# Cross-attention and MX feed-forward on one core: values stored by head pairs through five staging tiles, their attention buffer refilled in six parts

## The chip, the cores and the metric

The kernel runs on one core of a Trainium2 chip, as one launch. The metric is the device time of the whole program in microseconds, as the median of several runs. A profile of one execution gives the trace that is read here. In it PE is TensorE's matmul stream, PEld its weight loads, DVE is VectorE, ACT ScalarE, POOL GpSimd and SP SyncE, which here only issues DMAs; SPq and ACTq are the DMA issues of SP and ACT.

## The reference, cut to what matters

x has 2048 rows of 512 (tokens), ctx has 6404 rows of 512 (4 x 1601 keys), and there are 16 heads of 32.

```
q  = layernorm(x) @ Wq + bq          # 2048 x 512, times 1/sqrt(32)
kv = ctx @ Wkv + bkv                 # 6404 x 1024: keys, values
q, k = fake_quant(q), fake_quant(k)  # int8, one scale for each row and head
v = fake_quant(v, axis=keys)         # int8, one scale for each of the 512 columns,
                                     # max|v| over all 6404 keys / 127
a = softmax(q k^T);  a = fake_quant_unsigned(a)   # uint8, one scale for each row
x = x + (a @ v) @ Wp + bp
x = x + mx_ffn(layernorm(x))         # 512 -> 2048 -> 512, block-scaled int8
```

The scale of a value column is known only when all 51 tiles of keys have been seen: no value can be rounded before the last one is projected.

## The kernel before, in words

There are three functions, each a block of its own in which the five engines run their own instruction streams and meet at semaphores; all engines finish one block before the next begins.

**prepare** walks through a list `ITEMS` of 67 items: 51 key tiles of 128 ctx rows (`KT` = 51, the last has 4 rows) and 16 query tiles. Queries 0 to 7 stand between key tiles 22 to 36, one at every second tile; queries 8 to 15 come last. For an item i, PE turns the input (`turn_in(i+1)`), multiplies (`project(i)`: keys into `ps_k`, values into `ps_v`, four f32 products of 512 columns each) and turns the previous item's result (`turn_out(i-1)`). For a key tile VectorE adds the bias, quantises by head (`split`, lines 568 to 578), and adds the bias to the values (`take_values`, line 591). The quantised keys are written as three bf16 parts: ScalarE copies the first (468), GpSimd subtracts (358), ScalarE copies the second (470), GpSimd subtracts again (361); PE turns all three (418), ScalarE copies them to `stage` (496, 497) and SP stores a pair of tiles to DRAM (282).

Values stay in SBUF as f32, in `v32`, a view of the whole `arena` (51 x 512 words a partition). The largest |v| is found by `largest_values` at 13 places (`GROUPS`), each a strided reduction over two to five tiles (599) and a maximum with `v_scale` (600). SP also stores columns of heads 4 to 15 of each tile to `late_v_dram`, by head pairs (`store_late_values`, 286). Beside the tiles VectorE prepares the FFN weights in 8 pieces, one in four tiles: `powers` at tiles 1, 5, .. 29 (609), `weight_bytes` one tile later (618), `weight_values` two later (624), 2.28 us each; and the biases in four steps at tiles 4, 6, 8 and 10 (554 to 563). `bias`, `w` and their parts lie in places of the arena that value tiles take over later.

After the last key tile, GpSimd reduces `v_scale` across partitions (367), VectorE forms `inv_v` (683, `scale_of_values`, at query 9), and beside queries 10 to 13 VectorE multiplies heads 0 to 3 (`EARLY_HEADS` = 4) by it into bytes (678, `value_bytes`), ScalarE widens them to f16 (522) and SP stores them (340). Before the block ends SP waits for all its stores.

**attention** has 256 rows of work (16 heads x 16 tiles of 128 queries). For each row PE makes 6404 scores in five chunks (833), VectorE copies each chunk out of PSUM with its maximum (888), GpSimd forms the row's maximum and bias (995, 999, 1003), ScalarE takes exp in two halves (940) as a byte part `n8` and a 16-bit part `n16`, SP transposes both by DMA (816, 820), GpSimd unpacks the bytes (1010, 1011) and PE multiplies by the values, three rows (`LAG`) behind the scores, in four parts between the score chunks (846). ScalarE takes the output (946).

At the beginning ScalarE's queue loads keys, queries and values of heads 0 and 1; later, at rows 0 to 5 of each head, keys (240 and 160 KB pieces) and queries of the next one (`next_head`, 910 and 914). Heads 4 to 15 get their values in f32 from `late_v_dram`, two heads (1632 KB) in one DMA into `late_v` at row 14 of heads 2, 4, .. 12 (`RELOAD_AT`, 933), and GpSimd multiplies and rounds them into `v_head` in six parts at rows 7 to 12 of the head before (1041, 1043, `round_values`), both operations of a part in one row and after that row's unpack. `SUMS_AT`, `INVERT_AT` and `SCALE_AT` (rows 2, 5 and 6) place the softmax sums, their reciprocals (VectorE, 896) and the scaling of the previous head's output (GpSimd, 1030).

**finish** does the projection and the FFN; the change leaves it as it is.

## Time and profile before

| | us |
|---|---|
| median of 3 runs | 2727.17 |
| lowest, highest | 2725.52, 2740.77 |
| the profiled execution | 2737.58 |
| its span from first to last instruction | 2735.8 |
| prepare, up to the next block's first instruction | about 553.7 |
| attention, first to last score copy | 564.6 to 2430 |
| finish | to 2735.8 |

The span is 1.8 us less than the profiled execution's time. Of the span VectorE is busy 2492.6 us (91%), PE 2249.1 (82%), ScalarE 1983.4 (72%) and GpSimd 1419.5 (52%). The mean granted TensorE clock is 0.821 of full speed. A stretch in which one engine is busy nearly all the time is bound by that engine; in the others a chain through several engines sets the pace, and it has to be followed tile by tile. Idle time of an engine that does not set the pace costs nothing.

### The profile page before, as it was taken

The page shows a single profiled execution, that of the slowest core. Times are in us where ns is not written, and L with a number is a line of the kernel's source. Part 1 is how long each engine was busy: PE and PEld are TensorE (multiplying, and loading weights), DVE is VectorE, ACT ScalarE, POOL GpSimd, SP SyncE. Part 2 cuts the span into 40 slices and gives each one's busy share as a digit, 9 for nine tenths or more (in the row PEclk, how much of TensorE's full clock was granted, in tenths as well). Part 3 has the DMA queues.
Part 4 walks back from the last instruction along what each step waited for, and adds up shares of the span by engine and source line. Part 5 has one row for each costly group of instructions (what it writes and reads, how often), then busy time and mean ns, then how long its engine had stood idle before and what let it go on. Part 6 is the DMA issues. An engine that isn't in the chain of part 4 may idle for free. (4 is left out here: it accounts for less than half of the span.)

```text
span 2735.8 us, 52956 instructions
## 1 busy us (share of the span) xinstructions
PE 2249.1 (82%) x20003; PEld 1193.3 (44%) x20020; DVE 2492.6 (91%) x3592; ACT 1983.4 (72%) x1813; POOL 1419.5 (52%) x1855
## 2 busy tenths in 40 slices
PE   8899899968888888788888788888887777867886
PEld 4444454424444444444444444444444444433443
DVE  6998667879999999999999999999999999957997
ACT  3344333458888888888888888888988888864665
POOL 2432222136556575666757667675775758552001
PEclk9999999967677777777777876787777888779999
DMA  7565445489999999999999999999999999991000
GB/s 228 123 146 114 89 97 120 90 190 175 197 177 202 203 181 197 181 197 185 191 210 180 193 200 193 192 183 211 178 197 194 189 195 175 180 213 43 16 16 27
DMA packets 1389368, 442.13 MB, mean 162 GB/s; under 512 B 1323924, under 2 KB 1364372, under 8 KB 1387576
## 3 DMA queue, kind: packets, MB, share of 16 engines
q1 hardware_dynamic: 1378472, 397.08, 76.7%
q10 hardware_dynamic: 10736, 43.11, 6.3%
q8 instruction: 76, 1.25, 0.2%
q14 instruction: 84, 0.69, 0.1%
HBM read 78.99 MB, written 42.35 MB: 44 GB/s over the span
## 5 line engine op out<-in xcount | busy, mean ns | idle before, releaser
L888 DVE TENSOR_SCALAR_CACHE_REDUCE arena<-a_ps_s 128x1281 f32<-128x1281 f32 (+1 forms) x1280 | 1826.3, 1488 | 46.1 <-PE a_ps_s L833 38.1
L940 ACT ACTIVATE arena<-arena,a_bias,a_row_scale 128x3328 uint8<-128x3328 f32 (+1 forms) x512 | 1560.4, 3048 | 257.4 <-POOL a_bias L1003 255.7
L833 PE MATMUL a_ps_s<-arena,a_q_rep 96*128 96x512 bf16 (+2 forms) x3840 | 1232.4, 443 | 325.0 <-DVE arena L888 290.7
L846 PEld LDWEIGHTS a_ps_o<-a_v_head,a_nT 128*128 128x128 f16 x13056 | 529.6, 103 | 295.2 <-issue 160.9
L833 PEld LDWEIGHTS a_ps_s<-arena,a_q_rep 96*128 (+1 forms) x3840 | 314.6, 109 | 767.8 <-DVE arena L888 417.8
L1010 POOL CAST a_nT<-arena 128x1664 int16<-128x1664 uint8 x256 | 401.8, 1570 | 352.3 <-DMA arena<-arena 349.5
L846 PE MATMUL a_ps_o<-a_v_head,a_nT 128*128 128x32 f16 x13056 | 518.8, 183 | 43.4 <-POOL a_nT L1011 39.8
L1011 POOL CAST a_nT<-arena 128x1664 int16<-128x1664 uint8 x256 | 402.9, 1574 | 0.0
L358 POOL TENSOR_TENSOR p_rest<-p_kq,p_parts 128x512 f32<-128x512 f32 (+1 forms) x51 | 88.8, 1742 | 317.2 <-ACT p_parts L468 317.2
L999 POOL TENSOR_SCALAR a_row_max<-a_row_max,a_part_max 128x1 f32<-128x1 f32 x256 | 92.2, 360 | 246.6 <-DVE arena L888 229.3
L388 PE MATMUL p_ps_k<-p_wkv,p_ctxT 128*128 128x512 f32 (+1 forms) x408 | 190.3, 611 | 0.0
L388 PE MATMUL p_ps_v<-p_wkv,p_ctxT 128*128 128x512 f32 (+1 forms) x408 | 183.4, 592 | 0.0
L468 ACT ACTIVATE p_parts<-p_kq 128x512 bf16<-128x512 f32 (+1 forms) x51 | 32.1, 630 | 187.7 <-DVE p_kq L578 114.0
L1168 POOL TENSOR_TENSOR f_o<-arena,f_y 128x512 f32<-128x512 f32 x16 | 18.5, 1154 | 236.4 <-DVE f_y L1377 236.4
L388 PEld LDWEIGHTS p_ps_v<-p_wkv,p_ctxT 128*128 128x128 f32 (+1 forms) x408 | 76.7, 188 | 98.4 <-issue 98.2
L388 PEld LDWEIGHTS p_ps_k<-p_wkv,p_ctxT 128*128 128x128 f32 (+1 forms) x408 | 75.9, 197 | 78.1 <-issue 78.1
L568 DVE TENSOR_TENSOR p_kf<-p_ps_k,p_bkv 128x512 f32<-128x512 f32 (+1 forms) x51 | 35.2, 690 | 80.7 <-PE p_ps_k L388 80.1
L995 POOL TENSOR_SCALAR a_row_max<-a_part_max 128x1 f32<-128x1 f32 x256 | 93.6, 366 | 27.9 <-DVE arena L888 26.3
L888 DVE DVE_READ_ACCUMULATOR arena<-a_ps_s 128x1 f32 x1280 | 105.9, 83 | 0.0
L470 ACT ACTIVATE p_parts<-p_rest 128x512 bf16<-128x512 f32 (+1 forms) x51 | 32.1, 630 | 94.5 <-POOL p_rest L358 94.5
L940 ACT ACTIVATION_READ_ACCUMULATOR arena<-arena,a_bias,a_row_scale 128x1 f32 x512 | 95.7, 187 | 0.0
L1043 POOL TENSOR_SCALAR a_v_head<-a_late_v 128x256 f16<-128x256 f32 x72 | 82.8, 1150 | 6.7
(151 smaller groups left out, 1943.0 us busy)
## 6 DMA issues: line engine op xcount, KB each, us to landing
k_parts_transposed<-p_stage SPq DMA_DIRECT2D x25, 768.0 KB, 7.0
p_ctx<-in_ctx_dram SPq DMA_DIRECT2D x25, 512.0 KB, 5.8
arena<-k_parts_transposed ACTq DMA_DIRECT2D x48, 240.1 KB, 4.0
late_values<-arena SPq DMA_DIRECT2D x51, 192.0 KB, 6.9
a_late_v<-late_values ACTq DMA_DIRECT2D x6, 1632.0 KB, 9.6
arena<-in_L_ffn_W_dram SPq DMA_DIRECT2D x8, 1024.0 KB, 8.1
arena<-k_parts_transposed ACTq DMA_DIRECT2D x48, 160.1 KB, 3.8
a_q_rep<-q_transposed ACTq DMA_DIRECT2D x48, 128.0 KB, 5.4
```

The source lines that it names most:

```text
L358: nc.gpsimd.tensor_tensor(rest1[0:r, :], kq[0:r, :], parts[0:r, 0, :], ALU.subtract).then_inc(rest_ready, 1)
L388: last = nc.tensor.matmul(out, ctxT[:, i % 2, j, 0:r], weights[:, j], start=(j == 0), stop=(j == CC - 1))
L568: nc.vector.tensor_tensor(kf[0:r, :], ps_k[0:r, i % 2, :], bkv[0:r, 0:C], ALU.add).then_inc(k_taken, 1)
L833: last = nc.tensor.matmul(ps_s[:, b, n0:n0 + w], q, k_parts[0:3 * HD, slot, start[c] + n0:start[c] + n0 + w], start=True, stop=True)
L846: last = nc.tensor.matmul(ps_o[:, u, 0:HD], nT[:, u, j, :], v_head[:, v_slot, j, :], start=(j == 0), stop=(j == KT - 1))
L888: nc.vector.tensor_scalar(s_row[:, u, start[c]:start[c] + size[c]], ps_s[:, (u + c) % 2, 0:size[c]], 1.0, None, ALU.mult, ALU.max, accum_o ...
L940: nc.scalar.activation(out, s_row[:, u, keys_of_half[half]], ACT.Exp, scale=row_scale[:, u, 0:1], bias=bias[:, u:u + 1], accum_out=zsum[:, ...
L995: nc.gpsimd.tensor_scalar(m, part_max[:, u, 0:1], part_max[:, u, 1:2], part_max[:, u, 2:3], ALU.max, ALU.max).then_inc(three_done, 1)
L999: nc.gpsimd.tensor_scalar(m, m, part_max[:, u, 3:4], part_max[:, u, 4:5], ALU.max, ALU.max).then_inc(row_max_ready, 1)
L1010: nc.gpsimd.tensor_copy(low_T[u], bytes_T[:, u, :, 0])
L1011: nc.gpsimd.tensor_copy(high_T[u], bytes_T[:, u, :, 1]).then_inc(unpacked, 1)
L1043: nc.gpsimd.tensor_scalar(v_head[:, h % 2, tiles, :], some, ROUND, ROUND, ALU.add, ALU.subtract).then_inc(v_rounded, 1)
```

## The change

**Values.** `v32`, `GROUPS` and `late_values` go. A tile of values is written to one of five staging tiles (`v_tile`, `V_TILES` = 5) and stored whole, 512 columns as eight head pairs, to one DRAM tensor `v_dram` (`store_values`). ScalarE makes |v| of each tile (`vabs`, ACT.Abs) between its two copies of the key parts, and VectorE takes the maximum of it and `v_scale` one tile later (`largest_value`), 51 times. VectorE waits for the store and the Abs of tile t-5 before it writes tile t.

**Biases.** The third part is subtracted for one partition only, straight into `b_parts`: one copy less.

**Early heads.** `EARLY_HEADS` becomes 2. After all values are stored SP loads the first pair (`v_first`, 1632 KB) back; bytes are made at queries 10 and 11, ScalarE widens them straight into `v_head`, which together with `q_rep` now exists in both blocks. SP loads the keys of heads 0 and 1 at queries 9 and 10, the first half of their queries at 11 and 12, and head 0's second half at the end, before the block ends; `k_parts` moves to the beginning of the arena. `qiT` gets four tiles instead of two.

**Attention.** PE waits for 96 instead of 144 at heads 0 and 1, whose rows 4 to 15 are written out instead of looped, with a wait for the second half of the queries at row 8. The loads of heads 0 and 1 at the block's beginning shrink to the second half of head 1's queries; heads 2 and 3 load there as six parts. The reload becomes six DMAs of a sixth (272 KB), at rows 5, 7, 9, 11, 13 and 15 of heads 2, 4, .. 12. GpSimd does one of the 12 rounding operations in each of rows 3 to 14, before the row's unpack. The reciprocals move to row 7 and the scaling to row 15.

```diff
-EARLY_HEADS = 4
 GROUP = 2
+EARLY_HEADS = GROUP
...
+            def store_values(t):
+                sp.wait_ge(v_taken, t + 1)
+                sp.dma_start(v_dram[:, :, place(t), :].rearrange("g p c -> p g c"),
+                             v_tile[:, t % V_TILES, :].rearrange("p (g c) -> p g c", c=GROUP * HD)).then_inc(
+                                 v_stored[t % V_TILES], 16)
...
             for t in range(2 * PAIRS - 2, KT):
-                store_late_values(t)
+                store_values(t)
+            for i in range(V_TILES):
+                sp.wait_ge(v_stored[i], 16 * ((KT + V_TILES - 1 - i) // V_TILES))
+            sp.wait_ge(b_stored, 16)
+            sp.wait_ge(w_bytes, PIECES)
+            sp.dma_start(v_first.rearrange("p t c -> p (t c)"),
+                         v_dram[0].rearrange("p t c -> p (t c)")).then_inc(v_first_loaded, 16)
+
             for t in range(HALF_Q, QT):
-                if t > HALF_Q:
-                    store_query(t - 1)
...
+                store_query(t)
+                if t == HALF_Q + 1:
+                    sp.wait_ge(k_stored[0], 16 * ((PAIRS + 2) // 2))
+                    sp.wait_ge(k_stored[1], 16 * ((PAIRS + 1) // 2))
+                if HALF_Q + 1 <= t <= HALF_Q + 2:
+                    load_keys(t - HALF_Q - 1)
...
+                if HALF_Q + 3 <= t <= HALF_Q + 4:
+                    load_queries(t - HALF_Q - 3, 0, head_loaded[t - HALF_Q - 3])
+            for i in range(Q_TILES):
+                sp.wait_ge(q_stored[i], 16 * (QT // Q_TILES))
+            load_queries(0, 1, late_q_loaded[0])
...
                 nc.scalar.activation(parts[0:r, 0, :], kq[0:r, :], ACT.Copy).then_inc(hi_ready, 1)
+                act.wait_ge(v_taken, t + 1)
+                after_first(act, vmax_done, t - 1)
+                nc.scalar.activation(vabs[0:r, t % 2, :], v_tile[0:r, t % V_TILES, :], ACT.Abs).then_inc(vabs_ready, 1)
                 act.wait_ge(rest_ready, t + 1)
...
             def take_values(t):
                 r = rows(t)
-                if t == BIAS_TILE:
-                    dve.wait_ge(b_stored, 16)
-                if t == W_TILE:
-                    dve.wait_ge(w_turned, 2 * PIECES)
+                if t >= V_TILES:
+                    dve.wait_ge(v_stored[t % V_TILES], 16 * (t // V_TILES))
+                    dve.wait_ge(vabs_ready, t - V_TILES + 1)
...
-            def largest_values(t):
-
-                for first, last in GROUPS.get(t, ()):
-                    some = v32[:, first:last, :].rearrange("p t c -> p c t")
-                    dve.wait_ge(v_taken, t + 1)
-                    steps.then_wait(nc.vector.tensor_reduce(largest[:], some, AX.X, ALU.max, apply_absolute_value=True))
-                    steps.then_wait(nc.vector.tensor_tensor(v_scale[:], v_scale[:], largest[:], ALU.max))
...
+            def largest_value(t):
+                r = rows(t)
+                dve.wait_ge(vabs_ready, t + 1)
+                after_first(dve, vmax_done, t)
+                nc.vector.tensor_tensor(v_scale[0:r, :], v_scale[0:r, :], vabs[0:r, t % 2, :],
+                                        ALU.max).then_inc(vmax_done, 1)
...
-    ROUND_AT, ROUND_PARTS, RELOAD_AT = 7, 6, 14
...
+    ROUND_AT, ROUND_PARTS = 3, 6
+    RELOAD_AT = [ROUND_AT + 2 + 2 * part for part in range(ROUND_PARTS - 1)] + [QT - 1]
...
+            def load_late_values(group, part):
+
+                after_first(act, v_rounded, ((group - 1) * GROUP - 1) * ROUND_PARTS + part + 1 if group > 1 else 0)
+                tiles = slice(part * KT // ROUND_PARTS, (part + 1) * KT // ROUND_PARTS)
+                act.dma_start(late_v[:, tiles, :].rearrange("p t c -> p (t c)"),
+                              v_dram[group, :, tiles, :].rearrange("p t c -> p (t c)")).then_inc(late_v_loaded, 16)
...
             for row in range(ROWS):
-                maximum_and_unpack(row, row % 2)
-                head, part = row // QT + 1, row % QT - ROUND_AT
-                if EARLY_HEADS <= head < H and 0 <= part < ROUND_PARTS:
-                    round_values(head, part)
+                maximum(row, row % 2)
+                head, step = row // QT + 1, row % QT - ROUND_AT
+                if EARLY_HEADS <= head < H and 0 <= step < 2 * ROUND_PARTS:
+                    round_values(head, step)
+                if row >= 1:
+                    unpack(row - 1, 1 - row % 2)
```

## Rows read from the trace of the kernel before

**Rows 1.** Windows: stretch, its length, then busy us of PE, PEld, DVE, ACT, POOL.
```profile
56.75:207.56 150.81, 136.49 (x577) 71.02 (x576) 137.44 (x175) 66.09 (x92) 55.81 (x33) 0.95 0.59 136
207.56:395.77 188.21, 170.83 (x705) 88.39 (x704) 131.59 (x201) 74.72 (x114) 48.69 (x32) 0.96 0.48 104
395.77:509.31 113.54, 111.66 (x440) 54.25 (x438) 86.51 (x139) 42.37 (x71) 32.80 (x28) 1.00 0.49 101
564.62:2430.00 1865.38, 1518.43 (x16791) 825.08 (x16789) 1829.03 (x2575) 1599.87 (x1279) 1218.61 (x1706) 0.76 1.03 190
```

**Rows 2.** One line's view, L888 within attention (its waits), L820 (ns min/median/max).
```profile
  PE a_ps_s L833: 27.3, 21
...
L820 SPq DMA_TRANSPOSE a_nT<-arena x256: 3699/3828/11876, 580.2 to 2436.1; - x128
```

**Rows 3.** Timeline: start, us, instruction, [idle before]; SP and VectorE in attention.
```profile
1145.77 10.96 SPq L820 DMA_TRANSPOSE a_nT<-arena  x1
...
1161.01 1.49 DVE L888 TENSOR_SCALAR_CACHE_REDUCE arena<-a_ps_s 128x1281 f32<-128x1281 f32 x1 [5.66 <-PE a_ps_s L833]
```

**Rows 4.** Groups of instructions by line: busy us, mean ns, idle before, releaser.
```profile
L1010 POOL CAST a_nT<-arena 128x1664 int16<-128x1664 uint8 x256 | 401.8, 1570 | 352.3 <-DMA arena<-arena 349.5
L1043 POOL TENSOR_SCALAR a_v_head<-a_late_v 128x256 f16<-128x256 f32 x72 | 82.8, 1150 | 6.7
L599 DVE TENSOR_REDUCE p_largest<-arena 128x512 f32<-128x2048 f32 (+3 forms) x13 | 46.3, 3561 | 0.4
L470 ACT ACTIVATE p_parts<-p_rest 128x512 bf16<-128x512 f32 (+1 forms) x51 | 32.1, 630 | 94.5 <-POOL p_rest L358 94.5
L600 DVE TENSOR_TENSOR p_v_scale<-p_v_scale,p_largest 128x512 f32<-128x512 f32 x13 | 9.0, 693 | 0.4
L508 ACT ACT_TABLE_LOAD x1 | 1.3, 1283 | 0.0
```

**Rows 5.** Timeline of VectorE: the first instruction of key tiles 35 and 37.
```profile
374.84 0.69 DVE L568 TENSOR_TENSOR p_kf<-p_ps_k,p_bkv 128x512 f32<-128x512 f32 x1 [2.42 <-PE p_ps_k L388]
...
395.77 0.69 DVE L568 TENSOR_TENSOR p_kf<-p_ps_k,p_bkv 128x512 f32<-128x512 f32 x1 [2.42 <-PE p_ps_k L388]
```

**Rows 6.** Groups of PE by line, up to 505 us: its transposes of the key parts.
```profile
L418 PE MATMUL p_ps_t<-ident,p_parts 128*128 128x128 bf16 x596 | 44.3, 227 | 33.5 <-ACT p_stage L497 25.6 <-POOL p_parts L361 7.9
```

**Rows 7.** Timeline of PE in prepare: the same 12 transposes behind two waits.
```profile
130.53 0.84 PE L418 MATMUL p_ps_t<-ident,p_parts 128*128 128x128 bf16 x12 [0.92 <-ACT p_stage L497]
...
276.71 1.46 PE L418 MATMUL p_ps_t<-ident,p_parts 128*128 128x128 bf16 x12 [6.64 <-ACT p_stage L497]
```

**Rows 8.** Timeline of VectorE and GpSimd near tiles 7 and 8.
```profile
79.96 2.28 DVE L624 SCALAR_TENSOR_TENSOR arena<-arena,p_power 128x2048 bf16<-128x2048 int8 x1
...
80.06 3.20 POOL L358 TENSOR_TENSOR p_rest<-p_kq,p_parts 128x512 f32<-128x512 f32 x1 [3.12 <-ACT p_parts L468]
...
87.90 1.16 POOL L358 TENSOR_TENSOR p_rest<-p_kq,p_parts 128x512 f32<-128x512 f32 x1 [2.75 <-ACT p_parts L468]
```

**Rows 9.** One line's view, DMA landing: the last value stores (L286), then `late_v` (L933).
```profile
DMA to landing us min/median/max: 4.6/5.0/5.5
...
DMA to landing us min/median/max: 7.7/9.6/13.0
```

**Rows 10.** Timeline of SP's queue at the end of prepare.
```profile
514.11 2.02 SPq L286 DMA_DIRECT2D late_values<-arena  x3
```

**Rows 11.** Timeline of VectorE: end of prepare, beginning of attention.
```profile
524.52 1.86 DVE L678 TENSOR_TENSOR p_ctx<-arena,inv_v 128x1632 int8<-128x1632 f32 x1
...
545.88 0.69 DVE L664 TENSOR_TENSOR p_kf<-p_ps_k,p_bq 128x512 f32<-128x512 f32 x1 [0.87 <-PE p_ps_k L388]
...
553.73 0.16 DVE L892 MEMSET arena<- 128x124 uint32 x1 [2.43 <-PEq L57]
...
564.62 1.50 DVE L888 TENSOR_SCALAR_CACHE_REDUCE arena<-a_ps_s 128x1281 f32<-128x1281 f32 x1 [10.73 <-PE a_ps_s L833]
```

**Rows 12.** DMA issues of the page: KB each, median us to landing.
```profile
arena<-k_parts_transposed ACTq DMA_DIRECT2D x48, 240.1 KB, 4.0
```

More of the change, by code:

```diff
@@ L965, in rows_of_head @@
                         next_head(h + 1, 1 - slot, t)
+            later = slice(T // 2, T)
             for s in range(3):
-                for half in range(2):
-                    load(0, 0, s, half)
-            load_values(0, 0)
-            for s in range(3):
-                for half in range(2):
-                    load(1, 1, s, half)
-            load_values(1, 1)
+                act.dma_start(q_rep[s * HD:(s + 1) * HD, 1, later], q_dram[HD:2 * HD, later]).then_inc(late_q_loaded[1], 16)
+            for part in range(ROUND_PARTS):
+                load_late_values(1, part)
             act.dma_start(wp[:], A.wp.rearrange("(j p) n -> p j n", p=P)).then_inc(wp_loaded, 16)
@@ L1011, in unpack @@
                 nc.gpsimd.tensor_copy(high_T[u], bytes_T[:, u, :, 1]).then_inc(unpacked, 1)
-            def maximum_and_unpack(row, u):
-                maximum(row, u)
-                if not (isinstance(row, int) and row == 0):
-                    unpack(row - 1, 1 - u)
             def add_sums(h):
```

192 lines of the change are left out of this document (92 added, 100 removed).

## The prediction

> **What bounds the kernel.** I read the stretches first [rows 1]. The kernel has three parts: prepare up to about 553.6 us, attention from 564.6 to 2430, and the rest, which the change does not touch. In attention VectorE is busy 1829 of 1865 us: it copies each score chunk out of PSUM, and nothing in the change alters that. What can be won there is only what VectorE waits for PE inside it: 27.3 us in 21 waits [rows 2]. Two of them are over 5 us, each some rows after a 1632 KB reload of `late_v`; ahead of the one of 5.66 SP was 10.96 us at issuing one transpose [rows 3], whose median is 3.8 [rows 2]. GpSimd waited 352.3 us for transposes in all [rows 4], 1.4 a row.
>
> In prepare PE and VectorE share the bound. From 395.77 to 509.31 there are 14 key tiles, 8.1 us each. From 56.75 to 207.56 there are 16 tiles, where that pace would give 130 us and 150.81 were taken [rows 1]. Two tiles and a query take 20.93 us when undisturbed [rows 5]; the 16 tiles and 8 queries from 207.56 to 395.77 would take 167.4 at that pace and took 188.21. So 21 + 21 = 42 us are lost. PE waits in its transposes of the key parts 33.5 us [rows 6], the longer times behind tiles in which VectorE does its split, a grouped maximum of 3.6 us on average [rows 4] and a piece of the weights. PE also runs slower just after: the same 12 transposes take 1.46 us behind a wait of 6.64 and 0.84 behind one of 0.92 [rows 7], so a wait costs more than its length.
>
> **Part 1, the maximum of |v|.** Removed: 13 reductions, 46.3 us, and 13 small maxima of 693 ns, 9.0 us [rows 4]. Added on VectorE: 51 maxima of the same kind at 0.69, 35 us. VectorE so has 20 us less, and, more important, no tile with 3.6 to 5.4 us extra. In the first stretch it loses four such groups (of 4.7 or 3.8 us and 0.7 each, near 20 us) and gains 16 x 0.72 = 11.5: busy 137.4 becomes some 129 of a PE bound of 130. Bubbles remain, since the bias steps and weight pieces still make tiles of near 12 us: I take 140, 11 us less. In the second stretch VectorE's 131.6 busy us are far below 167; its two bad places are two reductions that each meet a weight piece, one with 6.64 us of PE waiting [rows 7]. I take 5 of the 21 us lost to stay: 16 less. After 395.77 there is little to win. Sum -27; from nothing (the chain is the bound, not VectorE) to -42 (everything lost comes back).
>
> Added on ScalarE: 51 Abs of 128x512. The nearest row is the copy of the same shape, 630 ns; ScalarE waits 94.5 us for GpSimd's difference right behind the place of the Abs [rows 4], 1.85 a tile, and the Abs fits in. It also waits for `v_taken`, which VectorE gives 0.7 us after the keys that ScalarE has just copied. Cost 0; if that cover were gone 51 x 0.63 = 32 us. Bound above: an Abs that needed a table load of 1.28 us [rows 4] before and after it: 2.6 us where 1.2 are free, 51 x 1.4 = 71. I take 0, since copies and a square root in prepare share one set. The Trainium skill ("ScalarE: Activation LUTs", Table sets) says that abs is in every set, so by it there is no load; no row here shows an Abs.
>
> Against the change: each new maximum has two SBUF inputs and falls on GpSimd's differences. GpSimd's subtraction takes 1.16 us beside a reduction, and 3.20 beside a VectorE operation of 2.28 us with two SBUF inputs [rows 8]; so a 0.69 us maximum can cost it 0.7. The chain from a key tile to PE's transposes (3.4 us split, copy 0.63, difference 1.2, copy 0.63, difference 1.2, handshakes) is about 8 us, PE's way to the same place (values, next keys and values, 3.6 each, and a transpose) 11.4. It holds 0.7 more, and with a weight piece (+2) just so. I charge nothing and keep up to 10 us of the gain as uncertain. The Trainium skill says the same ("GPSIMD Engine Reference", Key points: GpSimd shares its SBUF interfaces with VectorE, contention with instructions of two SBUF inputs); by it every tile pays the 0.7, and 51 x 0.7 = 36 us would be its worst, if PE waited for all of it.
>
> **Part 2, staging and stores.** Value tile t is overwritten by t+5 and stored about two tiles after it is made; the last three stores land in 4.6 to 5.5 us [rows 9], two or more tiles before the place is wanted. SP's store has a third more pieces; what is queued behind on SP (weights, queries, context) has tiles of slack. Cost 0; a store late by more than two tiles would stop VectorE. The bias edit drops one copy, counted as nothing.
>
> **Part 3, the end of prepare.** Before, VectorE makes head 0's bytes at 524.52 [rows 11]. Now they wait for all stores (the last issues end at 516.1 [rows 10], landing takes 5, a third larger: 522.3) and for a 1632 KB load. The nearest transfers of that size land in 7.7 to 13.0 us, beside transposes [rows 9]; here the queues are idle, so 8: 530.3. Behind VectorE's wait stand queries 11 to 15, and PE and ScalarE wait for those. Bytes 1.9 and query 11 to 535.3, bytes and query 12 to 540.2; PE comes from idle and is slow at first (I add 1.7, in the proportion of [rows 7]); then 4.2 a query: query 15 begins near 551.5 instead of 545.88 [rows 11]. That is +5.6, with 3 and 12 as bounds. SP issues three query loads before the barrier: +1. Two fewer heads of bytes are already inside.
>
> Then the gain: the block begins at 553.7 and the first score copy at 564.62, behind 10.73 us of waiting [rows 11]. PE's first products need about 1.3 us; heads 0 and 1 are now loaded before the barrier, by SP between the last queries. -9.4. Net 5.6 + 1 - 9.4 = -3; range -6 to +5.
>
> **Part 4, attention.** The 1632 KB transfer becomes six of 272 KB, at rows 5, 7, 9, 11, 13 and 15 of even heads. Each should hold the transposes a sixth of what the whole did, near 1.7 us instead of 10, and PE's lag of three rows absorbed 4 to 5 us of the large one. At row 5 it stands beside a key load of the next head; key pieces of 240 KB land in 4.0 us [rows 12] and the waits after them are 1.5 us at most. ScalarE issues it behind a wait on `v_rounded` that GpSimd has met one row before, so it blocks nothing. Rounding moves from both operations (a multiplication, and the rounding of 1.15 us [rows 4]) in six rows, after the unpack, to one in each of twelve, ahead of it: it falls into the 1.4 us a row in which GpSimd waits for the transpose. Heads 2 and 3 join: 24 operations of at most 1.15, under 28 us, hidden the same way. The scaling of a head moves from the crowded row 6 to row 15.
>
> Of 27.3 us about 18 follow a reload, 9 the key loads. I leave 10: -17, from -24 to 0. The Trainium skill ("DMA: Bandwidth & Descriptors", Rules for kernel authors) speaks against it: coalesce small transfers, at least 1 MiB for bandwidth. By that the six would hold the engines longer than the one; in rows: 6 x 4.0 = 24 us against 9.6.
>
> **Sum.** -27 - 3 - 17 = -47. The profiled execution took 2737.6 us and would take 2691; the median of the runs is 2727.2, so I forecast 2727 - 47 = 2680.
>
> **Rivals.**
> - *Chain (0.15).* GpSimd's stretched differences become PE's bound wherever a weight piece runs; prepare gives 8 instead of 27. For it: the 3.20 us of [rows 8]. Against: at those tiles the early chain already carries +2 without a PE wait. 2727 - 28 = 2699.
> - *Reload costs the same in pieces (0.12).* The 10 us of a reload are only spread, and the added traffic of heads 2 and 3 counts. -27 - 3 = -30: 2697.
> - *Six transfers cost more (0.05, the other side).* In each of 36 rows the transfer stops transposes for up to its whole 4.0 us landing. A row has 7.3 us (1865 / 256), SP's two transposes take 3.8 and, by my estimate, under half of that: some 5.5, so 1.8 are free; the rest, 2.2, comes to 36 x 2.2 = 79, less the 30 of the other parts: +49, 2776. It is slower than before when a transfer costs over 30 / 36 = 0.8 us. The coalescing rule above would lead here.
> - *First values late (0.05).* The load of the first pair takes 13 us and the stores land later: the end of prepare gives +5 instead of -3: 2688.
> - *The change moves nothing in prepare or attention (0.01).* 2724.
> - *The Abs loads tables (0.01).* 2680 + 71 = 2751.
>
> **Numbers.** The forecast holds 0.61. The range reaches from -72 (all bounds good: 42 + 6 + 24) cut to 2655, to 2708, which takes in the first two rivals and part of the worst; outside are about 2 in 10. A measurement of this kernel can tell about 1% (27 us) from no change. Faster by over 1%: the forecast, most of the late load, and over half of the first two rivals: 0.81. Within 1%: 0.14. Slower: 0.05.
>
> **What will show it.** Right: the first query after tile 50 starts near 482 instead of 509; no PE wait over 3 us in the key transposes; VectorE idle 5 to 8 us before head 0's bytes; first score copy 1.5 us after the block begins; VectorE's waits in attention near 10 us with none over 3; no transpose issue over 6 us. Wrong: GpSimd's differences with medians near 1.9 us and PE still waiting behind them; VectorE waiting at the value copy; waits of VectorE at rows 6 to 16 of even heads, one for each reload.

## The result, and the profile after

The changed kernel takes 2688.8 us (median of 4 runs, 2682.2 to 2691.2), the kernel before 2729.5 in the same series (4 runs, 2725.5 to 2740.8): ratio 0.984, 95% interval 0.9805 to 0.9876. It is 40.7 us faster, 1.5 %. Forecast were 47 us less, and 2680 us. In a second series the same two kernels had 2682.2 and 2725.1: 42.9 us less, ratio 0.9845 (0.980 to 0.9891).

The windows of the changed kernel, in the columns of [rows 1] (the last three numbers of a row are the granted clock, the share of the DMA engines and GB/s). The stretches are cut at the same work: key tiles 5 to 21, 21 to 37, 37 to the first query behind tile 50, the rest of prepare, attention, the rest of the program.

```profile
55.58:195.84 140.26, 134.73 (x581) 70.28 (x580) 133.34 (x182) 73.81 (x106) 55.80 (x32) 0.99 0.63 154
195.84:370.21 174.37, 164.35 (x702) 84.15 (x701) 129.38 (x209) 85.80 (x133) 50.93 (x33) 1.00 0.52 118
370.21:481.75 111.54, 111.50 (x440) 54.36 (x438) 80.09 (x145) 49.72 (x84) 34.16 (x28) 1.00 0.50 111
481.75:530.00 48.25, 32.69 (x132) 15.85 (x133) 30.70 (x63) 15.93 (x28) 2.05 (x3) 0.91 0.68 154
530.00:2381.00 1851.00, 1489.04 (x16791) 818.47 (x16789) 1827.13 (x2575) 1601.00 (x1279) 1238.69 (x1729) 0.79 1.06 192
```

Against [rows 1] the first two stretches (key tiles 5 to 21 and 21 to 37) are 10.6 and 13.8 us shorter, and PE's granted clock in them rose from 0.95 and 0.96 to 0.99 and 1.00; the third is 2.0 shorter. In attention VectorE is as busy as before (1827.13 against 1829.03); what it lost is idle time.

| stage, us | before | after | change | forecast |
|---|---|---|---|---|
| up to the query behind tile 50 | 509.31 | 481.75 | -27.6 | -27 |
| from there to the first score copy | 55.31 | 48.25 | -7.1 | -3 |
| attention, first score copy to its end | 1864.4 | 1849.7 | -14.6 | -17 |
| the rest | 306.8 | 306.4 | -0.4 | 0 |
| span | 2735.8 | 2686.2 | -49.6 | -47 |

The profiled executions differ by 49.6 and the medians by 40.7. The larger part of the difference is that the profiled execution of the kernel before lay above the median of its runs (experiment 12 profiles it again).

The end of prepare, from the timeline of VectorE of the changed kernel (start, us, instruction, idle before); compare [rows 11]:

```profile
499.67 1.86 DVE L696 TENSOR_TENSOR arena<-arena,inv_v 128x1632 int8<-128x1632 f32 x1 [2.60 <-DMA arena<-values]
...
519.39 0.69 DVE L681 TENSOR_TENSOR p_kf<-p_ps_k,p_bq 128x512 f32<-128x512 f32 x1 [0.88 <-PE p_ps_k L406]
...
528.79 0.16 DVE L917 MEMSET arena<- 128x124 uint32 x1 [3.37 <-PEq L57]
530.00 1.49 DVE L913 TENSOR_SCALAR_CACHE_REDUCE arena<-a_ps_s 128x1281 f32<-128x1281 f32 x1 [1.05 <-PE a_ps_s L853]
```

VectorE waits 2.60 us for head 0's values. Query 15 (519.39) begins 37.6 us behind the first query, before 36.6. The block begins at 528.79, and the first score copy waits 1.05 us instead of 10.73.

### The profile page after: what moved, and what is told of

The parts are those of the page before. It is cut to its first block and busy times, and to the rows that moved or that the text cites. A ratio compares the mean times of both kernels' runs of the same rounds, so it can differ in the third digit from the quotient of the medians.

```text
span 2686.2 us, 53043 instructions
## 1 busy us (share of the span) xinstructions
PE 2212.1 (82%) x20020; PEld 1181.0 (44%) x20020; DVE 2478.9 (92%) x3614; ACT 2009.7 (75%) x1862; POOL 1443.9 (54%) x1879
## 5 line engine op out<-in xcount | busy, mean ns | idle before, releaser
L913 DVE TENSOR_SCALAR_CACHE_REDUCE arena<-a_ps_s 128x1281 f32<-128x1281 f32 (+1 forms) x1280 | 1824.3, 1488 | 23.7 <-PE a_ps_s L853 16.6
L853 PE MATMUL a_ps_s<-arena,q_rep 96*128 96x512 bf16 (+2 forms) x3840 | 1201.6, 434 | 345.6 <-DVE arena L913 313.9
L853 PEld LDWEIGHTS a_ps_s<-arena,q_rep 96*128 (+1 forms) x3840 | 310.7, 108 | 782.8 <-DVE arena L913 456.5
L866 PEld LDWEIGHTS a_ps_o<-v_head,a_nT 128*128 128x128 f16 x13056 | 524.3, 102 | 263.6 <-issue 148.5
L866 PE MATMUL a_ps_o<-v_head,a_nT 128*128 128x32 f16 x13056 | 514.1, 182 | 28.9 <-POOL a_nT L1027 26.2
L1026 POOL CAST a_nT<-arena 128x1664 int16<-128x1664 uint8 x256 | 401.8, 1569 | 211.1 <-DMA arena<-arena 205.7
L376 POOL TENSOR_TENSOR p_rest<-p_kq,p_parts 128x512 f32<-128x512 f32 (+1 forms) x51 | 74.9, 1469 | 286.0 <-ACT p_parts L486 286.0
L1011 POOL TENSOR_SCALAR a_row_max<-a_part_max 128x1 f32<-128x1 f32 x256 | 93.8, 366 | 15.5 <-DVE arena L913 14.9
L379 POOL TENSOR_TENSOR p_parts<-p_rest,p_parts 128x512 bf16<-128x512 f32 (+1 forms) x51 | 81.0, 1588 | 37.7 <-ACT p_parts L491 37.7
L1057 POOL TENSOR_SCALAR v_head<-a_late_v 128x256 f16<-128x256 f32 x84 | 96.6, 1150 | 7.1
```

The costliest lines, as they stand in the source:

```text
L376: nc.gpsimd.tensor_tensor(rest1[0:r, :], kq[0:r, :], parts[0:r, 0, :], ALU.subtract).then_inc(rest_ready, 1)
L379: nc.gpsimd.tensor_tensor(parts[0:r, 2, :], rest1[0:r, :], parts[0:r, 1, :], ALU.subtract).then_inc(lo_ready, 1)
L853: last = nc.tensor.matmul(ps_s[:, b, n0:n0 + w], q, k_parts[0:3 * HD, slot, start[c] + n0:start[c] + n0 + w], start=True, stop=True)
L866: last = nc.tensor.matmul(ps_o[:, u, 0:HD], nT[:, u, j, :], v_head[:, v_slot, j, :], start=(j == 0), stop=(j == KT - 1))
L913: nc.vector.tensor_scalar(s_row[:, u, start[c]:start[c] + size[c]], ps_s[:, (u + c) % 2, 0:size[c]], 1.0, None, ALU.mult, ALU.max, accum_o ...
L1011: nc.gpsimd.tensor_scalar(m, part_max[:, u, 0:1], part_max[:, u, 1:2], part_max[:, u, 2:3], ALU.max, ALU.max).then_inc(three_done, 1)
```

## Experiments

Twelve kernels ran. `q8` is the start of the query behind tile 50. "Attention" goes from the first score copy to the end of the last. "Waits" are VectorE's idle time ahead of its score copies, behind the first copy; all but at most 0.6 us of each sum are waits for PE. "Time" is a median; kernels of one series share the runs of the kernel before: 2725.1 for experiments 1, 2, 4 and 5, 2732.6 for 6 to 9, 2724.8 for 3, 10 and 11, and 2726.2 for 12. The ratio is taken against these. The median of the same kernel before moves by 8 us between the series, so a few us between two kernels of different series say nothing; what a stage costs is read from the traces.

| kernel | q8 | first score copy | attention | waits | time | ratio |
|---|---|---|---|---|---|---|
| before | 509.3 | 564.6 | 1864.4 | 27.3 | 2729.5 | |
| 12 before, again | 508.2 | 563.5 | 1855.2 | 19.6 | 2726.9 | 1.000 (0.998 to 1.003) |
| after | 481.8 | 530.0 | 1849.7 | 16.0 | 2688.8 | 0.984 (0.981 to 0.988) |
| 1 changed, again | 483.3 | 531.9 | 1836.6 | 4.5 | 2682.2 | 0.985 (0.980 to 0.989) |
| 2 one reload | 483.1 | 531.4 | 1859.5 | 24.9 | 2697.3 | 0.989 (0.984 to 0.993) |
| 3 one reload, again | 482.4 | 529.7 | 1861.2 | 24.2 | 2701.8 (1 run) | |
| 4 rounding behind | 483.5 | 531.7 | 1844.6 | 12.2 | 2681.4 | 0.983 (0.979 to 0.987) |
| 5 reload later | 484.0 | 532.1 | 1839.5 | 6.8 | 2678.1 | 0.982 (0.978 to 0.986) |
| 6 maximum alone | 482.8 | 537.4 | 1853.3 | 17.7 | 2702.3 | 0.990 (0.983 to 0.997) |
| 7 no maximum | 483.5 | 531.8 | 1841.8 | 9.6 | 2679.0 (2 runs) | 0.980 (0.972 to 0.989) |
| 8 maximum ahead | 491.1 | 539.0 | 1839.0 | 5.4 | 2688.2 | 0.984 (0.977 to 0.990) |
| 9 loads in attention | 484.5 | 539.9 | 1847.9 | 13.0 | 2693.6 | 0.985 (0.978 to 0.991) |
| 10 weight halves | 489.7 | 537.0 | 1840.4 | 7.2 | 2686.8 | 0.986 (0.983 to 0.990) |
| 11 halves, reload later | 492.1 | 539.2 | 1835.5 | 3.4 | 2684.2 | 0.985 (0.983 to 0.988) |

### 1 to 3: the changed kernel again, and with one reload

Experiment 1 is the changed kernel unedited.

> The changed kernel itself, beside the experiments on one chip. Its first profile had VectorE waiting for PE 16 us within attention, 12.9 of them near row 8 of heads 4, 6, 8, 10 and 12 (2.21, 4.29, 1.23, 2.70, 2.51). If these come from a fixed meeting of transfers, a second profile shows waits at the same rows, 10 to 18 us in sum. If they are chance, they lie elsewhere. Ratio to the kernel before 0.984.

It has 4.5 us of waits, 1.8 of them near row 8 of even heads, where the first execution had 16.0 and 12.9: less than either theory had. The ratio repeats (0.9845). The waits of one execution are one sample, so they are compared below as groups.

Experiment 2 gives the reload back as one transfer of 1632 KB, at row 15 of even heads (the kernel before has it at row 14). The waits on it follow, and the first load of heads 2 and 3 is one transfer too; all else stays. Experiment 3 is the same kernel again.

```diff
-    RELOAD_AT = [ROUND_AT + 2 + 2 * part for part in range(ROUND_PARTS - 1)] + [QT - 1]
+    RELOAD_AT = [QT - 1]
...
-                tiles = slice(part * KT // ROUND_PARTS, (part + 1) * KT // ROUND_PARTS)
+                tiles = slice(0, KT)
```

> The changed kernel with the reload of a pair as one DMA of 1632 KB again, at row 15 of even heads; rounding stays spread over twelve rows. Theory (one large transfer holds up the transposes): waits of 4 to 7 us near row 2 of odd heads come back, waits near row 8 of even heads go, VectorE's waits in attention 25 to 30 us instead of 16, time +10 us. Rival (the spread rounding, not the split transfer, made attention shorter): waits stay near 16 us, time the same within 3.

> A second look at the changed kernel with one DMA of 1632 KB at row 15. Waits differ between executions of one kernel, so the sums have to be compared as groups: so far 27.3, 17.7 and 24.9 us with one transfer, and 16.0, 4.5, 12.2, 9.6, 5.4 and 13.0 with six. Theory: 18 to 28 us again, most of it at rows 2 to 4 of odd heads. Rival (the groups overlap by chance): under 14.

The waits are back, 24.9 us against 4.5, and the time with them: 2697.3 (2694.3 to 2699.8) against 2682.2 (2678.7 to 2691.4), 15 us. The third kernel repeats it: 24.2 us. In both they lie behind the reload again, at rows 2 to 4 of the odd heads (about 17 and 16 us of the sum); in the kernel before, whose reload is one row earlier, they begin at row 1. The worst of them, in the timeline of SP's queue, ScalarE's queue, PE and VectorE of experiment 3:

```profile
1578.00 0.34 ACTq L953 DMA_DIRECT2D a_late_v<-values  x1
1581.83 10.52 SPq L840 DMA_TRANSPOSE a_nT<-arena  x1
...
1594.82 0.53 PE L866 MATMUL a_ps_o<-v_head,a_nT 128*128 128x32 f16 x13 [6.61 <-POOL a_nT L1026]
...
1596.54 1.49 DVE L913 TENSOR_SCALAR_CACHE_REDUCE arena<-a_ps_s 128x1281 f32<-128x1281 f32 x1 [6.71 <-PE a_ps_s L853]
```

The transfer is issued at 1578.00, the next long transpose takes SP 10.52 us instead of its median of 3.85, GpSimd's unpacked row is late, PE waits 6.61 and VectorE 6.71. The part of the change that pays in attention is the six transfers, not the spread rounding. Experiments 1 and 2 share a series, and their runs don't overlap.

### 4: rounding behind the unpack

```diff
+                if row >= 1:
+                    unpack(row - 1, 1 - row % 2)
                 head, step = row // QT + 1, row % QT - ROUND_AT
                 if EARLY_HEADS <= head < H and 0 <= step < 2 * ROUND_PARTS:
                     round_values(head, step)
-                if row >= 1:
-                    unpack(row - 1, 1 - row % 2)
```

> The changed kernel with each rounding step behind the row's unpack instead of ahead of it. Theory (the step only fills GpSimd's wait for the transpose, and GpSimd has time either way): GpSimd's wait before the unpack goes from 206 us back to about 330, and the time moves by less than 3 us. Rival (the place of rounding is worth part of the gain): VectorE's waits in attention grow from 16 to 25 us, time +8.

No difference: 2681.4 (2677.9 to 2684.3) against 2682.2. GpSimd's wait ahead of its unpack is 343.5 us here and 211.1 in the changed kernel, where the rounding lies inside it; VectorE notices neither.

### 5: reload later

The waits left over in the first profile of the changed kernel lie near row 8 of even heads: 12.9 of the 16.0 us. The largest, from the timeline:

```profile
1269.99 0.34 ACTq L953 DMA_DIRECT2D a_late_v<-values  x1
...
1270.37 0.59 ACTq L935 DMA_DIRECT2D arena<-k_parts_transposed  x1
1271.00 0.82 ACTq L939 DMA_DIRECT2D q_rep<-q_transposed  x1
...
1273.00 8.47 SPq L840 DMA_TRANSPOSE a_nT<-arena  x1
...
1281.02 1.57 POOL L1026 CAST a_nT<-arena 128x1664 int16<-128x1664 uint8 x1 [6.85 <-DMA arena<-arena]
...
1285.96 1.49 DVE L913 TENSOR_SCALAR_CACHE_REDUCE arena<-a_ps_s 128x1281 f32<-128x1281 f32 x1 [4.29 <-PE a_ps_s L853]
```

The reload's first piece (row 5) goes out 0.4 us ahead of a key load and 1.0 ahead of a query load of the next head. The transpose behind all three takes 8.47 us, and VectorE waits 4.29 us, three rows on. So the pieces were moved to rows with fewer loads beside them:

```diff
-    RELOAD_AT = [ROUND_AT + 2 + 2 * part for part in range(ROUND_PARTS - 1)] + [QT - 1]
+    RELOAD_AT = [7, 9, 10, 12, 14, 15]
```

> The changed kernel with the six reloads at rows 7, 9, 10, 12, 14 and 15 instead of 5, 7, 9, 11, 13 and 15, so that none stands beside a key load of rows 0 to 5. Theory (the waits near row 8 of even heads come from the reload at row 5 on top of the key loads, and from the one at row 7 before the backlog is gone): these waits fall from 12.9 us to under 4, time 8 to 10 us less than the changed kernel. Rival (each reload costs by itself wherever it stands): the waits move with the reloads to rows 10 to 15 and keep their sum.

The waits near row 8 are 0.2 us here and 1.2 in experiment 11; in the seven executions with a piece at row 5 they lie between 1.8 and 12.9. 6.8 us remain in all, spread over other rows. Forecast were 8 to 10 us less time. The time is 2678.1 (2677.2 to 2680.4), the lowest of all, but its 4 us below experiment 1 are within that one's own spread: the waits near row 8 are gone, a gain in time isn't shown.

### 6: the maximum alone

Part 1 of the change put into the kernel before: Abs on ScalarE, a maximum per tile on VectorE; staging, end of prepare and attention as before.

```diff
+                nc.scalar.activation(vabs[0:r, t % 2, :], v32[0:r, place(t), :], ACT.Abs).then_inc(vabs_ready, 1)
...
-                    steps.then_wait(nc.vector.tensor_reduce(largest[:], some, AX.X, ALU.max, apply_absolute_value=True))
-                    steps.then_wait(nc.vector.tensor_tensor(v_scale[:], v_scale[:], largest[:], ALU.max))
+                nc.vector.tensor_tensor(v_scale[0:r, :], v_scale[0:r, :], vabs[0:r, t % 2, :],
+                                        ALU.max).then_inc(vmax_done, 1)
```

> The kernel before with the maximum of |v| by tile alone (Abs on ScalarE, one maximum on VectorE in each tile), everything else as before. Theory: this is the whole gain in the key tiles: the first query after the last key tile starts at 482 to 485 us instead of 509.3, attention keeps its 27 us of waits, time -25 us. Rival (staging tiles, w-waits and the bias edit also carry part of it): it starts at 490 or later, time -15 or less.

q8 lies at 482.8: the whole gain of the key tiles is this part's, and staging, stores and the bias edit carry nothing, as forecast. The time is 30 us below the kernel before, where 25 were expected; attention has 17.7 us of waits and not 27, which is in the spread of the kernel before itself (experiment 12).

### 7 and 8: how much the new maximum still costs

Experiment 7 lets the maximum work on one column of 512 and leaves the others out of the scales (`v_scale` starts at 1 there). Each of the 51 maxima still takes 0.16 us instead of 0.69. Experiment 8 puts the maximum of tile t - 1 ahead of tile t's split instead of behind its values.

```diff
-                nc.vector.tensor_tensor(v_scale[0:r, :], v_scale[0:r, :], vabs[0:r, t % 2, :],
+                nc.vector.tensor_tensor(v_scale[0:r, 0:1], v_scale[0:r, 0:1], vabs[0:r, t % 2, 0:1],
...
-            nc.vector.memset(v_scale[:], 0.0).then_inc(set_up, 1)
+            nc.vector.memset(v_scale[:], 1.0).then_inc(set_up, 1)
```

> The changed kernel with the per-tile maximum over one column instead of 512, so that v_scale is left out of the computation; Abs stays. It gives the floor of what the maximum costs. Theory (VectorE's load in the first 16 tiles still sets them): tiles 5 to 21 take 130 to 133 us instead of 140.3, tiles 21 to 37 167 to 170 instead of 174.4, GpSimd's second difference falls from 1.59 to about 1.2 us. Rival (what is left there is the bias steps and the weight pieces): tiles 5 to 21 stay at 137 or more.

```diff
+                if t >= 1:
+                    largest_value(t - 1)
                 split(t)
                 take_values(t)
-                if t >= 1:
-                    largest_value(t - 1)
```

> The changed kernel with the maximum of tile t-1 at the beginning of tile t, ahead of its split, instead of behind its values: VectorE does the same work, but GpSimd's second difference no longer meets it in light tiles. Theory (contention with GpSimd is hidden by the chain's slack): L379's mean falls from 1588 to about 1250 ns and the key tiles end within 2 us of before. Rival (the contention is on PE's path): the key tiles end 5 to 8 us earlier.

Both expectations missed. Without the maximum tiles 5 to 21 take 137.3 instead of 140.9 (130 to 133 were expected), tiles 21 to 37 take 177.7 instead of 174.4, and q8 is where it was: 27 us less of VectorE's work won nothing. With the maximum ahead, tiles 5 to 21 take 140.4, tiles 21 to 37 182.0, and q8 is 7.7 us late. GpSimd's second difference fell there as expected, from 1588 to 1351 ns, but the first rose from 1469 to 1686. The timelines of one place, tile 22, show why. First the changed kernel:

```profile
208.63 0.68 DVE L618 TENSOR_TENSOR p_v_scale<-p_v_scale,arena 128x512 f32<-128x512 f32 x1
...
208.98 1.35 POOL L376 TENSOR_TENSOR p_rest<-p_kq,p_parts 128x512 f32<-128x512 f32 x1 [5.44 <-ACT p_parts L486]
209.23 3.24 DVE L635 SCALAR_TENSOR_TENSOR arena<-arena,p_inverse 128x2048 int8<-128x2048 f32 x1
...
210.36 0.63 ACT L491 ACTIVATE p_parts<-p_rest 128x512 bf16<-128x512 f32 x1 [0.94 <-POOL p_rest L376]
...
211.07 2.42 POOL L379 TENSOR_TENSOR p_parts<-p_rest,p_parts 128x512 bf16<-128x512 f32 x1 [0.74 <-ACT p_parts L491]
...
213.63 0.83 PE L436 MATMUL p_ps_t<-ident,p_parts 128*128 128x128 bf16 x12 [1.58 <-POOL p_parts L379]
```

and the same place in experiment 8, where no maximum stands between the values and the weight piece:

```profile
210.61 2.28 DVE L635 SCALAR_TENSOR_TENSOR arena<-arena,p_inverse 128x2048 int8<-128x2048 f32 x1
...
210.71 3.20 POOL L376 TENSOR_TENSOR p_rest<-p_kq,p_parts 128x512 f32<-128x512 f32 x1 [5.79 <-ACT p_parts L486]
...
213.94 0.63 ACT L491 ACTIVATE p_parts<-p_rest 128x512 bf16<-128x512 f32 x1 [2.58 <-POOL p_rest L376]
...
214.65 1.16 POOL L379 TENSOR_TENSOR p_parts<-p_rest,p_parts 128x512 bf16<-128x512 f32 x1 [0.74 <-ACT p_parts L491]
...
216.89 1.35 PE L436 MATMUL p_ps_t<-ident,p_parts 128*128 128x128 bf16 x11 [3.46 <-ACT arena L518]
```

These rows fit one rule: whichever engine starts first runs at its own pace, and the other stands until it ends. In experiment 8 VectorE starts at 210.61 and needs 2.28; GpSimd, starting at 210.71, ends at 213.91, 1.0 us after VectorE. In the changed kernel GpSimd starts first (208.98; its 1.35 holds the rest of the maximum, and it ends at 210.33). VectorE's weight operation shows 3.24 and ends at 212.47, 2.1 us after GpSimd; GpSimd's second difference, which starts at 211.07, shows 2.42 and ends 1.0 after VectorE.

What it does to PE goes through ScalarE, which works in a fixed order: it waits for GpSimd's first difference (0.94 us in one, 2.58 in the other) before it copies PE's earlier transposes out to `stage`, and in experiment 8 that copy is what PE waits for. PE waits 1.58 in one and 3.46 in the other, and its twelve transposes take 0.83 in one, eleven of them 1.35 in the other. The 0.69 us maximum behind the values lets ScalarE's copy finish and GpSimd start ahead of the weight piece. It pays for itself by its place.

Over the whole of prepare the order is this. In the changed kernel 15 of the 16 weight operations start behind GpSimd and show 3.24 us. In experiments 7 and 8 three of 16 do, and in the kernel before none. In tiles 5 to 21 the order costs nothing that shows: experiment 8 takes 140.4 us there and experiment 1 140.9. The loss is in tiles 22, 26 and 30, where a weight piece and a query stand in one tile, and in the tiles behind two of them. Experiment 8 also begins each split 0.69 us later, which can be part of its 7.7 us; experiment 7 does not, and its tiles 22, 26 and 30 are long as well (16.8, 15.2 and 14.9 us against 13.8). The medians can't show it: 2688.2 has the ratio 0.984 (0.977 to 0.990), that of the changed kernel.

### 9: the first loads inside attention

```diff
-                if HALF_Q + 1 <= t <= HALF_Q + 2:
-                    load_keys(t - HALF_Q - 1)
...
+            for h in range(2):
+                for s in range(3):
+                    act.dma_start(k_parts[s * HD:(s + 1) * HD, h, :],
+                                  k_dram[s, h * HD:(h + 1) * HD, :]).then_inc(head_loaded[h], 16)
...
```

The queries of both heads move in the same way.

> The changed kernel with keys and queries of heads 0 and 1 loaded by ScalarE's queue at the beginning of attention, as in the kernel before, instead of by SP beside the last queries. Theory: the first score copy waits 10 us for PE again instead of 1.05; the block begins 1 to 1.5 us earlier; time +8 to +9 us. Rival (the loads in the tail held up stores that the barrier waits for, so their removal pays for itself): the block begins 5 us or more earlier, time +4 or less.

The beginning of the block and of the score copies, from this kernel's timeline of VectorE:

```profile
530.38 0.16 DVE L912 MEMSET arena<- 128x124 uint32 x1 [2.14 <-PEq L57]
539.92 1.49 DVE L908 TENSOR_SCALAR_CACHE_REDUCE arena<-a_ps_s 128x1281 f32<-128x1281 f32 x1 [9.39 <-PE a_ps_s L848]
```

The wait is back. The block begins 9.4 us after query 15 in experiment 1 and 8.2 here, and the first score copy 9.54 us behind the block instead of 1.2: the prefetch gives 8.3 us and costs 1.2 (forecast 9.4 and 1). The time is 11 us above experiment 1's, but in another series: against the kernel before of its own it is 39 us less, where experiment 1 has 43. The stage shows the price; the medians put it between 4 and 11 us.

### 10 and 11: weight pieces in halves

If one VectorE instruction holds GpSimd for its whole length, halves should let it in between. Both operations of a piece (L635 and L641 of the changed kernel) were cut in two; experiment 11 adds the later reload.

```diff
+                for a in range(2):
+                    s = slice(a * B // 2, (a + 1) * B // 2)
+                    last = nc.vector.scalar_tensor_tensor(blocks(wq8)[:, s], blocks(w[n % 2])[:, s], 32.0,
+                                                          over(inverse[:, s], MX), ALU.mult, ALU.mult)
...
```

> The changed kernel with VectorE's two operations of a weight piece (2.28 us, two SBUF inputs) each cut into two halves of about 1.2 us. The runs so far show VectorE's weight operation and GpSimd's difference excluding each other for whole instructions: the one that starts first is normal, the other long (3.20 of 1.16, or 3.24 of 2.28). Theory (the interface is held for one instruction): with halves GpSimd's second difference falls from 2.42 to 1.2 to 1.7 us where it meets one, PE's waits behind it (1.6, 1.9, 1.4) shrink to under 1, and the key tiles end 3 to 6 us earlier. Rival (it is held while VectorE has such work at all, or alternates): differences stay at 2.4 or more and nothing moves; the two extra starts cost 16 x 0.06 us.

> The halves together with the reloads at rows 7, 9, 10, 12, 14 and 15. A second look at the later reload: waits at rows 8 to 9 of even heads under 1 us in sum again (0.24 in the first look, 12.9, 1.8, 6.9, 2.3 and 11.4 with the reload at row 5), VectorE's waits in attention 5 to 9 us. If both effects add, 2672 to 2678 us where the changed kernel has 2682 to 2689. Rival (the first look was luck): waits at row 8 of even heads come back, over 4 us.

The groups of the changed kernel up to 482 us (busy us, mean ns, idle before):

```profile
L379 POOL TENSOR_TENSOR p_parts<-p_rest,p_parts 128x512 bf16<-128x512 f32 (+1 forms) x51 | 81.0, 1588 | 37.7 <-ACT p_parts L491 37.7
L376 POOL TENSOR_TENSOR p_rest<-p_kq,p_parts 128x512 f32<-128x512 f32 (+1 forms) x51 | 74.9, 1469 | 286.0 <-ACT p_parts L486 286.0
L436 PE MATMUL p_ps_t<-ident,p_parts 128*128 128x128 bf16 x600 | 41.9, 220 | 15.4 <-POOL p_parts L379 10.4 <-ACT arena L518 5.0
...
L489 ACT ACTIVATE arena<-arena 128x512 f32<-128x512 f32 (+1 forms) x51 | 31.7, 622 | 2.8 <-DVE arena L611 1.3
L641 DVE SCALAR_TENSOR_TENSOR arena<-arena,p_power 128x2048 bf16<-128x2048 int8 x8 | 25.9, 3244 | 0.0
L635 DVE SCALAR_TENSOR_TENSOR arena<-arena,p_inverse 128x2048 int8<-128x2048 f32 x8 | 25.0, 3124 | 0.0
```

and of experiment 10 up to 490 us:

```profile
L378 POOL TENSOR_TENSOR p_rest<-p_kq,p_parts 128x512 f32<-128x512 f32 (+1 forms) x51 | 74.6, 1463 | 312.2 <-ACT p_parts L489 312.2
L381 POOL TENSOR_TENSOR p_parts<-p_rest,p_parts 128x512 bf16<-128x512 f32 (+1 forms) x51 | 63.1, 1238 | 37.7 <-ACT p_parts L494 37.7
L640 DVE SCALAR_TENSOR_TENSOR arena<-arena,p_inverse 128x1024 int8<-128x1024 f32 x16 | 34.2, 2177 | 0.0
L650 DVE SCALAR_TENSOR_TENSOR arena<-arena,p_power 128x1024 bf16<-128x1024 int8 x16 | 34.2, 2176 | 0.0
```

GpSimd got in: its second difference fell from 1588 to 1238 ns. But each half took 2.18 us where half of 2.28 is 1.14. Each of the 32 halves starts while one of GpSimd's differences (1.16) has 1.1 us to go, and ends 1.1 us after it; VectorE pays 68.4 us for pieces that cost 50.9 in the changed kernel. PE's waits in the key transposes grow from 15.4 to 21.8 us, and the key tiles end 6.4 us later than in experiment 1, where 3 to 6 us earlier were expected. By the medians it is 5 us slower (2686.8 against 2682.2 of another series), which is not clear of noise. Experiment 11 takes 2684.2, not the expected 2672 to 2678: its waits in attention are the fewest of all, 3.4 us, with 1.2 near row 8 of even heads (under 1 was expected), and q8 is 2.4 us later still than in 10.

### 12: the kernel before, again

> The kernel before, profiled a second time. By the medians the change is worth some 41 to 43 us, by the two profiled executions 49.6, and the first profiled execution of the kernel before was 8 to 10 us above the median of its runs. Theory 'luck in attention': the stages of prepare repeat within 1 us (tiles 5 to 21 in 150.8, 21 to 37 in 188.2, query 8 at 509.3, the first score copy near 564.6), and attention is near 1854 to 1861 with waits of VectorE of 18 to 25 instead of 1864.4 with 27.3, so the span falls by 4 to 10 us. Theory 'luck in prepare': query 8 starts 3 us or more earlier than 509.3, so that the key tiles' gain of 27.6 read from one execution is too large.

Prepare repeats: 150.7 and 188.1 for the first two stretches, against 150.8 and 188.2; q8 1.1 us earlier. Attention is 9.2 us shorter, 7.7 of it waits, and the span 11.0, a little more than the 4 to 10 expected. The stages of prepare can be read from one execution, attention can't.

## Why the prediction was right, and where it was not

**Sum and range.** Forecast -47; measured -40.7 and -42.9 by medians. With the executions of both kernels averaged (before twice, changed twice) the spans are 2730.3 and 2681.6: -48.7. Both profiled executions of the changed kernel lie at or below the median of their runs, and before's first one above; on average before's two are 3.9 us above their medians (2737.6 and 2726.7 against 2729.5 and 2726.9) and the changed kernel's two 2.1 below (2688.0 and 2678.7 against 2688.8 and 2682.2), which makes 6 of the 6 to 8 us between traces and medians. The forecast subtracted 47 us from the median, though the sum had been made against an execution 10 us above it. The term for attention was the one in which that mattered.

**Key tiles, -27 forecast, -27.6 found (-25.8 between the means of two executions of before and six of kernels with the same prepare).** Experiment 6 shows that the new maximum alone makes this gain. The first stretch was forecast at 140 and took 140.3, and there the mechanism is the one named: reductions taken out of tiles 8, 9, 16 and 17. Experiment 8, in which VectorE's pieces go ahead of GpSimd as in the kernel before, has the same gain. VectorE's busy time was forecast at 129 us there and is 133.3, since its weight operations now stand behind GpSimd.

The second stretch was forecast at 172 and took 174.4, and there the number is partly luck. The prediction named two bad places, "two reductions that each meet a weight piece, one with 6.64 us of PE waiting". The reductions are in tiles 24, 25, 29 and 33, and the 6.64 us lie in tile 26, which has a weight piece and a query and no reduction. From the timeline of the kernel before, ahead of the row 276.71 of [rows 7]:

```profile
270.44 2.28 DVE L618 SCALAR_TENSOR_TENSOR arena<-arena,p_inverse 128x2048 int8<-128x2048 f32 x1
270.54 3.19 POOL L358 TENSOR_TENSOR p_rest<-p_kq,p_parts 128x512 f32<-128x512 f32 x1 [9.16 <-ACT p_parts L468]
...
273.76 0.63 ACT L470 ACTIVATE p_parts<-p_rest 128x512 bf16<-128x512 f32 x1 [3.30 <-POOL p_rest L358]
```

This is the picture of tile 22 in experiment 8. The lengths of the tiles, from VectorE's first instruction to its first of the next tile:

| tile | has | before | after | 7 no maximum | 8 maximum ahead |
|---|---|---|---|---|---|
| 22 | piece, query | 16.8 | 13.8 | 16.8 | 16.6 |
| 25 | reduction (before) | 12.2 | 8.8 | 8.3 | 8.9 |
| 26 | piece, query | 17.4 | 13.8 | 15.2 | 16.5 |
| 29 | reduction (before) | 11.8 | 8.3 | 8.0 | 8.4 |
| 30 | piece, query | 16.1 | 13.8 | 14.9 | 14.7 |

Nearly 9 us of the gain are in tiles 22, 26 and 30, 7 in tiles 25 and 29, and the others give 2 back in sum. With the order of before and no reduction left, 7.6 of the stretch's 13.8 us are gone again in experiment 8, and 3.3 in experiment 7. So between a quarter and somewhat over half of this stretch's gain comes from the order in which VectorE and GpSimd start (experiment 8 has its later splits in its figure). The prediction had no term for that.

PE's wait in its key transposes fell from 33.5 [rows 6] to 15.4 us. One wait is above 3 us where none was expected, 4.29 at 121.8 behind GpSimd. The 51 Abs take 622 ns each behind 2.8 us of waiting in all, as the copy's row [rows 4] let expect; prepare has two table loads, as before, and none of them stands at an Abs. ScalarE's wait for GpSimd's difference shrank from 94.5 to 48.5 us around them. The Trainium skill ("ScalarE: Activation LUTs", Table sets) says that abs is in every set. The trace agrees.

**Rival "chain".** It put GpSimd's stretched differences in PE's way and 8 us of gain. Its number was wrong, but its mechanism was at work already in the kernel before. The step that dismissed it, that at the weight pieces "the early chain already carries +2 without a PE wait", is wrong: behind the stretched differences of tiles 22, 26 and 30 PE waited 2.45, 6.64 and 5.81 us. GpSimd's second difference is indeed slower in the changed kernel, 1588 ns against 1244 for L361 before, but the first is faster, 1469 against 1742 for L358. The prediction counted the 0.7 us maximum as a cost alone. Experiments 7 and 8 show that its place behind the values also decides who starts first, and experiment 7 that cost and gain cancel: 3.6 us lost in the first stretch and 3.3 won in the second. That "I charge nothing" came true is this balance. The Trainium skill has the rule in "SBUF — State Buffer", Who interferes with whom: a VectorE instruction with two SBUF inputs and a GpSimd instruction that reads SBUF exclude each other for the whole instruction, and the order of issue decides who blocks. The rows of tile 22 agree, in both directions.

**End of prepare, -3 forecast, -7.1 found.** The step that failed is the delay of query 15: +5.6 was forecast, with 3 as the lower bound; +1.1 came. The load of 1632 KB was issued at 492.8, where the forecast's stores would have let it go at 494.7 (522.3 less the 27.6 of the key tiles), and landed in 6.8 us instead of 8. So VectorE waited 2.60 instead of 5.8, and from query 13 on it waits for PE again (1.27 us at 510.60), so that VectorE's lateness no longer counts: the delay was made up but for 1.1 us. The barrier took 1.6 more (1 forecast), the first score copy 9.7 less (9.4 forecast). Experiment 9 shows the last two.

**Attention, -17 forecast, -14.6 in the first pair.** The mean of the kernels with one transfer (before twice, experiments 2, 3, 6) is 1858.7 us with 22.7 of waits, that of the kernels with six at the original rows (after, 1, 4, 7 to 10) 1842.9 with 9.7: 15.8 us, of which 13.0 are waits; where the other 2.8 are no row shows. Experiments 2 and 3 alone, which differ from the changed kernel in the transfers only, have 1860.3 and 24.6. Forecast were waits of 27.3 down to 10, and they are 9.7 on average: the size was right, though the first profile by itself had 16.0. The rival that the cost is only spread falls with experiments 2 and 3. That six cost more falls too: pieces of 288 KB land in 4.0 us and those of 256 KB in 3.7, as the key pieces of [rows 12] had led to expect, and attention is shorter. The Trainium skill's rule to coalesce ("DMA: Bandwidth & Descriptors", Rules for kernel authors) would lead the other way. Here the single transfer of 1632 KB does land in 8.0 us (median, experiment 3), the six in 23 in sum, and the single one is the slower choice: the transposes beside it are what VectorE ends up waiting for. Two signs were too clean: waits above 3 us and transposes above 6 us do occur (up to 4.29 and 8.47; eight transposes are above 6, nine in the kernel before, up to 11.88), the worst where the first piece meets the key and query loads of the next head. The kind of wait named as the sign of failure, at rows 6 to 16 of even heads, is what remains; experiment 5 removes those near row 8.

**GpSimd's rounding, 0 forecast, 0 found.** Its wait for the transposes fell from 352.3 [rows 4] to 211.1 us; experiment 4 shows that even the order beside the unpack doesn't matter.

## What to carry to other kernels

If one large transfer runs beside small ones that the bound engine waits for, try it in pieces, even where the pieces take longer in all, and put them where no other load goes out. If VectorE and GpSimd meet at a place, look at who starts first there, and not only at the sum of busy time: a short operation in the right place can cost nothing, and taking it away can win nothing. When a forecast names a bad place, look up which instructions stand in it; here the number came out, and half of the places were others. And read a stage that repeats within 1 us from one execution, but one that lives on waits for transfers from several.

## What the runs showed of the hardware

VectorE's operation with two SBUF inputs (2.28 us) and GpSimd's difference (1.16 us) don't share. The one that started first showed its own length, and the other ended about its own length after it: GpSimd 1.0 us after VectorE (3.20 in all), VectorE 2.1 us after GpSimd (3.24 in all). Cutting VectorE's operation in two doubled the number of turns it had to wait for: 2.18 us a half.

VectorE's waits in attention summed to between 17.7 and 27.3 us in five executions with one transfer, and between 4.5 and 16.0 in seven with six at the original rows. The kernel before itself had 27.3 us with 6.37 as the longest in one execution, 19.6 with 7.79 in the other.
